# dt*u*B of two or four states a unit made by ScalarE and TensorE, more products with C on GpSimd, and Wout loaded by halves

## The chip, the cores and the metric

The kernel runs on one core of a Trainium2 chip. The metric is the device time of one execution in microseconds. In the text VectorE, ScalarE, GpSimd, TensorE and SyncE are the engines; SyncE only issues the transfers.

## What is computed

For x of 4 batches by 512 positions by 512 features: a layer norm, then `x + mamba(xn) + ffn(xn)`. The part around the change is the state recurrence of mamba, cut here to its core:

```python
dA = exp(A * dt)                  # per channel (1024), position (512) and state n (16)
dBu = (dt * Bm) * hs              # dt*u times B of the state, u = hs
h = dA_t * h + dBu_t              # a scan over the positions
y = sum over n of h * C
y = (y + hs * D) * silu(gate)
out = y @ Wout.T
```

The FFN is a gated one in fp8: `gelu(x@w0) * (x@w1)`, again to fp8, times w_linear.

## The kernel before, in words

There are two stages with a barrier between them. `block_a` makes the layer norm, the projections, the convolution, dt and dt*u, and leaves dt, dt*u and u*D of each unit (128 channels of one batch) in DRAM (`unit_d`), and B and C (`bc_d`). `block_b` runs 32 units, b of 4 by k of 8, in Python loops that are written out in full. A tile is 128 channels by 512 positions. For each of the 16 states n of a unit:

- ScalarE makes exp(A*dt) into one of four PSUM tiles `da[n % 4]` (L887). Before it waits till state n-4 has left that tile: when VectorE has made its product, or, where GpSimd makes it, when the scan is done.
- GpSimd makes dt*u*B into `dbu`, a ring of 8 tiles (L928), up to 8 states ahead of the scans.
- VectorE scans (L985). The result goes in place into `da`, or into `hp` for the states of `POOLED` = 1, 4, 7, 9, 12.
- The product with C is VectorE's (`prod`, L954, made behind the next state's scan) for 11 states, and GpSimd's (`hp` in place, L939, three states behind its dt*u*B) for the 5 of `POOLED`.
- TensorE transposes each product with four 128x128 matmuls and sums them in PSUM (`yT`, L1104), behind a skip term (L1119); GpSimd's products are taken 4 states later (`PE_LAG`).

The rest is placed by hand between the states. ScalarE, at state 6 of the next unit (`SWITCH`), copies yT (L856), makes the Silu of the gate (L877) with a table load on each side; TensorE turns y back (`BACK`, step 4); VectorE multiplies both at state 7 (`GATED`, L960, written y2). TensorE makes the FFN's products (L1062) in steps given by `FFN`, the gate's (L1074), and Wout in two halves of channels: `out_a` (first four units) in units 5 to 7 and `out_b` (last four) in units 0 to 3 of the next batch (L1026). A piece placed at -3 runs ahead of the unit's skip term. TensorE has two banks `mm` for all of them. ScalarE copies the FFN's banks at states 10 to 15 (L895) and makes the Gelu at state 1 of the next unit, between two table loads (L867, L868); VectorE multiplies and clips at state 4 (L1000, L1003), and GpSimd waits for that clip ahead of its product for state 4 (`PORT_GIVEN`), so that it is idle during the two bf16 instructions. VectorE adds out_a and out_b into `acc` (L966, L972) at states given by `OUT_A_ADDED` and `OUT_B_ADDED` (15 in unit 0, 5 in units 1 to 3). Units 1 to 5 have FFN work of that kind on VectorE.

SyncE's queue loads the next unit, the gate's and the FFN's weights while a unit runs, and in unit 7 the B and C tiles of the next batch, each behind a wait for its last reader. Wout is loaded once, 2 MB.

## Time and profile before

| | |
|---|---|
| median of 3 runs | 1150.81 us (1149.45 to 1151.9) |
| the profiled execution | 1151.44 us, its span 1149.7 us |
| VectorE busy | 1041.4 us, 91% |
| GpSimd busy | 926.6 us, 81% |
| TensorE busy (matmuls) | 932.7 us, 81% |
| ScalarE busy | 784.8 us, 68% |
| mean granted TensorE clock | 0.922 |
| first stage, to the barrier | about 240 us |

The page of the profile gives busy time and share for each engine over the span, then groups of instructions with their count, mean duration and the idle time of the engine ahead of them. A busy share is a mean over both stages. A timeline lists the instructions in order of time, several of one kind merged into a row, with the idle time ahead of the row in brackets and what ended it.

### The profile page before, as it was taken

What the parts mean: (1) busy time and instruction counts of PE and PEld (TensorE: products, weight loads), DVE (VectorE), ACT (ScalarE), POOL (GpSimd) and SP (SyncE); (2) the same over time, 40 slices, a digit from 0 to 9 for tenths busy, and PEclk for the clock granted to TensorE, in tenths of its full rate; (3) what the DMA queues carried; (4) which work ended last, traced back from release to release, by engine and by line L of the source; (5) the groups of instructions that cost most, each with busy time, mean ns of one, the idle gap of its engine ahead of it and who ended that gap; (6) DMA issues with size and microseconds to landing.
All of it is one profiled execution on the core that took longest, in us unless ns stands there. A gap on an engine that the chain in (4) does not pass through costs nothing.

```text
span 1149.7 us, 14675 instructions
## 1 busy us (share of the span) xinstructions
PE 932.7 (81%) x4304; PEld 573.4 (50%) x4304; DVE 1041.4 (91%) x1237; ACT 784.8 (68%) x1117; POOL 926.6 (81%) x751
## 2 busy tenths in 40 slices
PE   4979798747777798888887988887988788787988
PEld 3746465424444455555444555554545545454554
DVE  6958778579999999999999999999999999999994
ACT  3878887647777755767785557777846577787551
POOL 5333424389999999989999999999989989999991
PEclk9999999967998899899988998899889899989899
DMA  7566767983111217522212183321213922212100
GB/s 279 204 240 219 266 220 265 341 329 116 51 55 38 83 37 224 206 87 72 80 51 83 43 288 137 116 74 56 83 37 102 326 81 69 74 46 74 37 1 37
DMA packets 53158, 150.24 MB, mean 131 GB/s; under 512 B 5728, under 2 KB 14048, under 8 KB 50016
## 3 DMA queue, kind: packets, MB, share of 16 engines
q1 hardware_dynamic: 53088, 149.41, 37.7%
q8 instruction: 32, 0.52, 0.2%
q14 instruction: 38, 0.31, 0.1%
HBM read 111.37 MB, written 38.01 MB: 130 GB/s over the span
## 4 chain that ended last, share of the span: by engine, by line
POOL 52%; DVE 13%; issue 7%; PE 5%; ACT 0%; DVEq 0%; POOLq 0%
POOL dbu L928 38%; POOL hp L939 14%; DVE da L985 3%; DVE prod L954 3%; DVE hp L985 3%; PE mm L1026 2%; DVE gate_bf L1000 2%; DVE act L1003 2%; PE yT L1104 1%; PE mm L1083 1%; PE da L1026 1%; PE mm L1074 1%; ACT da L887 0%; DVE y L960 0%; ACT gate_bf L895 0%
## 5 line engine op out<-in xcount | busy, mean ns | idle before, releaser
L887 ACT ACTIVATE da<-unit,neg_a 128x512 f32<-128x512 f32 x512 | 340.2, 685 | 263.1 <-DVE prod L954 256.7
L928 POOL TENSOR_TENSOR dbu<-unit,b_head 128x512 f32<-128x512 f32 x384 | 478.0, 1280 | 3.5 <-POOLq L99 3.5
L985 DVE TENSOR_TENSOR_SCAN da<-da,dbu 128x512 f32<-128x512 f32 x352 | 418.3, 1217 | 7.7 <-POOL dbu L928 6.5
L1104 PE MATMUL yT<-ident,prod 128*128 128x128 f32 x1408 | 238.2, 298 | 150.4 <-DVE prod L954 149.8
L1104 PEld LDWEIGHTS yT<-ident,prod 128*128 128x128 f32 x1408 | 174.8, 151 | 282.1 <-DVE prod L954 242.1
L939 POOL TENSOR_TENSOR hp<-hp,c_head 128x512 f32<-128x512 f32 x128 | 163.6, 1278 | 59.0 <-DVE act L1003 45.9
L985 DVE TENSOR_TENSOR_SCAN hp<-da,dbu 128x512 f32<-128x512 f32 x160 | 193.4, 1209 | 7.9 <-ACT da L887 7.9
L954 DVE TENSOR_TENSOR prod<-da,c_head 128x512 f32<-128x512 f32 x256 | 171.3, 669 | 0.0
L928 POOL TENSOR_TENSOR dbu<-unit,b_all 128x512 f32<-128x512 f32 x128 | 160.4, 1280 | 0.0
L1062 PE MATMUL mm<-xn_b,w_sb 128*128 128x512 fp8e4 x512 | 151.6, 432 | 4.4 <-ACT gate_bf L895 3.3
L1074 PE MATMUL mm<-xnT_b,wgate 128*128 128x512 f32 x256 | 127.9, 597 | 1.8 <-ACT gate_bf L895 1.7
L1026 PE MATMUL mm<-y,wout_sb 128*128 128x512 f32 x240 | 111.9, 594 | 0.6 <-ACT gate_bf L895 0.6
L1104 PE MATMUL yT<-ident,hp 128*128 128x128 f32 x640 | 104.5, 290 | 0.0
L286 POOL TENSOR_TENSOR hs_lo<-hs,hs_hi 128x512 fp32r<-128x512 f32 x32 | 43.5, 1363 | 69.5 <-ACT hs_hi L465 69.5
L1062 PEld LDWEIGHTS mm<-xn_b,w_sb 128*128 128x128 fp8e4 x512 | 54.1, 110 | 63.4 <-issue 33.9
L289 POOL TENSOR_TENSOR dt_du<-dt_du,hs 128x512 f32<-128x512 f32 x32 | 41.1, 1284 | 53.8 <-DVE dt_du L405 53.4
L1104 PEld LDWEIGHTS yT<-ident,hp 128*128 128x128 f32 x640 | 82.4, 151 | 0.0
L350 DVE SCALAR_TENSOR_TENSOR conv<-proj,cols_sb,conv 128x511 f32<-128x511 f32 (+2 forms) x96 | 71.5, 747 | 8.8 <-ACT conv L446 6.3
L1083 PE MATMUL mm<-act,w_sb 128*128 128x512 fp8e4 x256 | 71.4, 416 | 0.0
L954 DVE TENSOR_TENSOR prod<-da,c_all 128x512 f32<-128x512 f32 x96 | 64.7, 675 | 0.0
L520 PE MATMUL proj<-xnT_lo,win_hi 128*128 128x512 f32 x128 | 55.8, 436 | 8.2 <-ACT xnT L427 4.3
L1026 PEld LDWEIGHTS mm<-y,wout_sb 128*128 128x128 f32 x240 | 42.9, 190 | 39.1 <-issue 36.7
(107 smaller groups left out, 1248.2 us busy)
## 6 DMA issues: line engine op xcount, KB each, us to landing
unit<-unit_d SPq DMA_DIRECT2D x32, 768.0 KB, 4.3
unit_d<-dt_du SPq DMA_DIRECT2D x32, 512.0 KB, 2.8
wf<-in_wffn SPq DMA_DIRECT2D x12, 1024.0 KB, 5.9
c_head<-bc_d SPq DMA_DIRECT2D x24, 512.0 KB, 5.0
b_head<-bc_d SPq DMA_DIRECT2D x18, 512.0 KB, 5.2
unit_d<-hsd SPq DMA_DIRECT2D x32, 256.0 KB, 3.9
w_sb<-w_d SPq DMA_DIRECT2D x64, 128.0 KB, 3.3
wgate<-in_win_gate SPq DMA_DIRECT2D x32, 256.0 KB, 2.7
```

The costliest lines, as they stand in the source:

```text
L350: ins = nc.vector.scalar_tensor_tensor(out=conv[:, k % 2, back:L], in0=proj[k % 3][:, 0:L - back], scalar=cols_sb[:, k, C_TAP + TAPS - 1 - ...
L520: nc.tensor.matmul(bank, hi, low, start=start, stop=False)
L887: nc.scalar.activation(da[n % SLOTS][:, :], unit[:, k % 2, 0, :], ACT.Exp, scale=neg_a[:, k, n:n + 1]).then_inc(da_ready, 1)
L928: nc.gpsimd.tensor_tensor(dbu[:, n % DBUS, :], unit[:, k % 2, 1, :], b_all[n // NS][:, n % NS, :], ALU.mult).then_inc(dbu_ready, 1)
L939: nc.gpsimd.tensor_tensor(hp[:, i % HPS, :], hp[:, i % HPS, :], c_all[m // NS][:, m % NS, :], ALU.mult).then_inc(hp_ready, 1)
L954: nc.vector.tensor_tensor(prod[:, slot, :], da[n % SLOTS][:, :], c_all[n // NS][:, n % NS, :], ALU.mult).then_inc(prod_ready, 1)
L985: nc.vector.tensor_tensor_scan(state, da[n % SLOTS][:, :], dbu[:, n % DBUS, :], 0.0, ALU.mult, ALU.add).then_inc(scanned, 1)
L1026: return nc.tensor.matmul(bank[:, :], wout_sb[:, c, h * P:(h + 1) * P], y2[:, c, :], start=(c == first), stop=(c == KU // 2 - 1))
L1062: ins = nc.tensor.matmul(bank[:, :], wffn[:, k % 2, j, f, s, :].bitcast(FP8), xn8[:, f, :].bitcast(FP8), start=(f == 0), stop=(f == HT - 1))
L1074: ins = nc.tensor.matmul(bank[:, :], wgate[:, k % 2, c * P:(c + 1) * P], xnT[:, c, :], start=(c == 0), stop=(c == 3))
L1083: ins = nc.tensor.matmul(bank[:, :], wlin[:, i, h * P:(h + 1) * P].bitcast(FP8), act8[:, i, :].bitcast(FP8), start=(i == 0), stop=(i == HI ...
L1104: ins = nc.tensor.matmul(yT[k % 2][:, t * P:(t + 1) * P], product[:, t * P:(t + 1) * P], ident[:, :], start=False, stop=last, is_transpose ...
```

## The change

A class `Ring` counts slots and semaphore values, now that the states of a kind differ from unit to unit. Units 0, 6 and 7 are LIGHT, 1 to 5 HEAVY. In a HEAVY unit GpSimd makes 6 products with C (states 0, 2, 4, 7, 9, 12) and 14 dt*u*B; in a LIGHT one 7 (0, 2, ..., 12) and 12. The dt*u*B of states 8 and 12 (HEAVY) or 4, 7, 10 and 13 (LIGHT) is made another way: TensorE turns dt*u of the next unit (`turn_u`, at its step 11) in the free yT bank, ScalarE copies it to `u_T` behind exp 15, and, one state ahead of each such state, multiplies it with B, which then is a value for each partition, in four 128x128 instructions (`scale_u`); TensorE turns the result into the PSUM tile of the state, four steps ahead (`turn_scaled`). exp(A*dt) of such a state goes to a tile in SBUF (`decay`, two of them) and its scan reads that and the PSUM tile. B turned (`bT_all`) is made at the end of each batch of the first stage. `prod` has 7 tiles for 8, `hp` 6 for 5. Wout has room for one half, and the halves are loaded in turn: the first at unit 4, the second at unit 7 of each batch. The diff, cut:

```diff
@@ -46,15 +46,49 @@
 WINS = 4
 DTS = 4
 SWITCH, GATED, GELU = 6, 7, 1
-DBUS = 8
-POOLED = (1, 4, 7, 9, 12)
-POOL_LAG, PE_LAG = 3, 4
-HPS = 5
-Y, M = len(POOLED), N - len(POOLED)
-OWN = tuple(n for n in range(N) if n not in POOLED)
-PRODS = 8
-ADDED = {n: [m for m in POOLED if min(m + PE_LAG, N - 1) == n] for n in range(N)}
-
+DBUS, PRODS, HPS, DECAYS, SCALED = 8, 7, 6, 2, 1
+POOL_LAG, PE_LAG, Z_AHEAD = 3, 4, 1
+LIGHT, HEAVY = (0, 2, 4, 6, 8, 10, 12), (0, 2, 4, 7, 9, 12)
+POOLED = (LIGHT, HEAVY, HEAVY, HEAVY, HEAVY, HEAVY, LIGHT, LIGHT)
+FEW, MANY = (8, 12), (4, 7, 10, 13)
+BY_SCALE = (MANY, FEW, FEW, FEW, FEW, FEW, MANY, MANY)
+
+
+def others(states):
+    return tuple(tuple(n for n in range(N) if n not in states[k]) for k in range(KU))
+
+
+class Ring:
+
+
+    def __init__(self, states, size):
+        self.states, self.size = states, size
+        self.order = [(k, n) for k in range(KU) for n in states[k]]
+        self.total = len(self.order)
+
+    def slot(self, k, n):
+        return self.order.index((k, n)) % self.size
...
+            return self.order[i - self.size], False
+        return [at for at in self.order if self.slot(*at) == self.slot(k, n)][-1], True
+
+
+OWN, BY_POOL = others(POOLED), others(BY_SCALE)
+PROD, HP, DBU, SCALE = Ring(OWN, PRODS), Ring(POOLED, HPS), Ring(BY_POOL, DBUS), Ring(BY_SCALE, SCALED)
+DECAY = Ring(BY_SCALE, DECAYS)
+ADDED = [{n: [m for m in POOLED[k] if min(m + PE_LAG, N - 1) == n] for n in range(N)} for k in range(KU)]
 
 
...
 FFN, FFN_COPIED = (5, 5, 5, 5, 4), (10, 10, 10, 10, 8)
 OUT_B, OUT_B_ADDED = (11, -3, -3, -3), (15, 5, 5, 5)
 GATE = (12, 11, 11, 11, 12, 12, 12, 10)
+U_T, U_T_COPIED = 11, 15
...
@@ -582,6 +625,14 @@
                     project_dt(k)
                     if k in (2, 5) and not last:
                         project(b + 1, k // 3)
+                if not last:
+                    pe.wait_ge(xnT_ready, b * HT + HT + HT - 1 + 2)
+                else:
+                    pe.wait_ge(bT_copied, B)
+                pe.sem_inc(waited, 1)
+                for t in range(LT):
+                    ins = nc.tensor.transpose(tp[0][:, t * 2 * N:(t + 1) * 2 * N], bc[:, t * P:(t + 1) * P], ident[0:2 * N, 0:2 * N])
+                ins.then_inc(bT_mm, 1)
 
             run_batches(pe, body)
...
@@ -766,6 +833,9 @@
                 sp.dma_start(w8_sb[:, :].rearrange("p (c n) -> p c n", c=HID // P * H // CHUNK),
                              w8_d[HID // P // 2:CHUNKS, :, :].rearrange("c p n -> p c n")).then_inc(wlin_loaded, 16)
 
+            def load_wout(half):
+                sp.dma_start(wout_sb[:, :, :], wout[:, half * KU // 2:(half + 1) * KU // 2, :]).then_inc(wout_loaded, 16)
+
             def load_xnT(b):
                 sp.dma_start(xnT[:, :, :].rearrange("p k l -> p (k l)"), row(xnT_d, b)).then_inc(xnT_loaded, 16)
...
+                if k == HT and not opening and b > 0:
+                    wait(out_b_mm, b * HT + HT)
+                    load_wout(0)
+                if k == KU - 1:
+                    wait(out_a_mm, b * HT + HT)
+                    load_wout(1)
...
         def _(act):
-            def sum_of(u, k):
-
-                act.wait_ge(hp_used, u * Y + Y + HPS)
+            def sum_of(b, k):
+
+                act.wait_ge(hp_used, HP.until(b, k + 1) + HP.total)
                 nc.scalar.activation(y_t[:, :], yT[k % 2][:, :], ACT.Copy).then_inc(y_t_ready, 1)
+
+            def copy_u(u, k):
+
+                act.wait_ge(u_T_mm, u + 1)
+                nc.scalar.activation(u_T[:, :], yT[k % 2][:, :], ACT.Copy).then_inc(u_T_ready, 1)
+
+            def scale_u(b, k, n, opening):
+
+                act.wait_ge(u_T_ready, b * KU + k + 1)
+                act.wait_ge(bT_ready, b + 1)
+                act.wait_ge(*slot_left(SCALE, dbu_mm, b, k, n))
+                for t in range(LT):
+                    ins = nc.scalar.activation(scaled[:, SCALE.slot(k, n), t * P:(t + 1) * P], u_T[:, t * P:(t + 1) * P], ACT.Copy,
+                                               scale=bT[:, t, n:n + 1])
+                ins.then_inc(scaled_ready, 1)
 
             def body(b, k, opening):
                 u = b * KU + k
...
+                    if n == 1 and first:
+                        copy_u(0, 0)
+                    if n == 1 and k == 0:
+                        nc.scalar.activation(bT[:, :, :].rearrange("p (o t) n -> p o t n", o=1),
+                                             bT_all[:, 0:1, :, :] if opening else bT_all[:, bass.ds(b, 1), :, :],
+                                             ACT.Copy).then_inc(bT_ready, 1)
+                    if n + Z_AHEAD in BY_SCALE[k]:
+                        scale_u(b, k, n + Z_AHEAD, opening)
+                    target = da[n % SLOTS][:, :]
+                    if n in BY_SCALE[k]:
+                        target = decay[:, DECAY.slot(k, n), :]
+                        if not (opening and DECAY.before(k, n)[1]):
+                            act.wait_ge(*scanned_before(DECAY, b, k, n))
+                    elif n >= SLOTS:
+                        act.wait_ge(*state_left(b, k, n - SLOTS))
+                    elif k > 0:
+                        act.wait_ge(*state_left(b, k - 1, n - SLOTS + N))
+                    elif not opening:
+                        act.wait_ge(*state_left(b - 1, KU - 1, n - SLOTS + N))
+                    nc.scalar.activation(target, unit[:, k % 2, 0, :], ACT.Exp,
                                          scale=neg_a[:, k, n:n + 1]).then_inc(da_ready, 1)
+                    if n == U_T_COPIED and not (isinstance(b, int) and b == B - 1 and k == KU - 1):
+                        copy_u(u + 1, (k + 1) % KU)
                     if k < FFN_UNITS and 0 <= n - FFN_COPIED[k] < 2 * HIDS[k]:
 
...
-                    nc.gpsimd.tensor_tensor(dbu[:, n % DBUS, :], unit[:, k % 2, 1, :], b_all[n // NS][:, n % NS, :], ALU.mult).then_inc(dbu_ready, 1)
+                    if n in BY_POOL[k]:
+                        if k == 0 and (n % NS == 0 or n - 1 not in BY_POOL[k]):
+
+                            if n >= G_AHEAD * NS:
+                                pool.wait_ge(b_loaded[n // NS], b * 16 + 16)
+                            elif not opening:
+                                pool.wait_ge(b_loaded[n // NS], b * 16)
+                            elif n == 0:
+                                pool.wait_ge(b_head_loaded, 16 * (B - 1))
+                        if not (opening and DBU.before(k, n)[1]):
+                            pool.wait_ge(*scanned_before(DBU, b, k, n))
...
+                        nc.gpsimd.tensor_tensor(dbu[:, DBU.slot(k, n), :], unit[:, k % 2, 1, :], b_all[n // NS][:, n % NS, :],
+                                                ALU.mult).then_inc(dbu_ready, 1)
+                    if 1 <= k <= FFN_UNITS and n == PORT_GIVEN:
+                        pool.wait_ge(act8_ready, b * FFN_UNITS + k)
...
@@ -976,16 +1086,19 @@
                 first = opening and k == 0
                 for n in range(N):
                     dve.wait_ge(da_ready, u * N + n + 1)
-                    dve.wait_ge(dbu_ready, u * N + n + 1)
                     state = da[n % SLOTS][:, :]
-                    if n in POOLED:
-                        i = POOLED.index(n)
-                        dve.wait_ge(hp_used, u * Y + i + 1)
-                        state = hp[:, i % HPS, :]
-                    nc.vector.tensor_tensor_scan(state, da[n % SLOTS][:, :], dbu[:, n % DBUS, :], 0.0,
-                                                 ALU.mult, ALU.add).then_inc(scanned, 1)
-
-                    if n > 0 and n - 1 in OWN:
+                    given = state, dbu[:, DBU.slot(k, n), :] if n in BY_POOL[k] else None
+                    if n in BY_POOL[k]:
+                        dve.wait_ge(dbu_ready, DBU.count(b, k, n))
+                    else:
+                        dve.wait_ge(dbu_mm, SCALE.count(b, k, n) + SCALE.total)
+                        given = decay[:, DECAY.slot(k, n), :], state
+                    if n in POOLED[k]:
...
@@ -1042,6 +1155,22 @@
                     if name != "out_b" and not (opening and wrapped):
                         break
                 return mm[bank]
+
+            def turn_u(b, k):
+
+                pe.wait_ge(unit_loaded[k % 2], unit_loads(b, k))
+                for t in range(LT):
+                    ins = nc.tensor.transpose(yT[k % 2][:, t * P:(t + 1) * P], unit[:, k % 2, 1, t * P:(t + 1) * P], ident[:, :])
+                ins.then_inc(u_T_mm, 1)
+
+            def turn_scaled(b, k, n):
+
+                pe.wait_ge(scaled_ready, SCALE.count(b, k, n))
+                pe.wait_ge(*state_left(b, k, n - SLOTS))
+                for t in range(LT):
+                    ins = nc.tensor.transpose(da[n % SLOTS][:, t * P:(t + 1) * P], scaled[:, SCALE.slot(k, n), t * P:(t + 1) * P],
+                                              ident[:, :])
+                ins.then_inc(dbu_mm, 1)
 
             group_bank = {}
...
+                        pe.wait_ge(prod_ready, PROD.count(b, k, n))
+                        add_state(k, prod[:, PROD.slot(k, n), :], False).then_inc(prod_used, 1)
+                    for m in ADDED[k][n]:
+                        pe.wait_ge(hp_ready, HP.count(b, k, m))
+                        add_state(k, hp[:, HP.slot(k, m), :], m == POOLED[k][-1]).then_inc(hp_used, 1)
+                    if n + SLOTS in BY_SCALE[k]:
+                        turn_scaled(b, k, n + SLOTS)
+                    if n == U_T and not (isinstance(b, int) and b == B - 1 and k == KU - 1):
+                        if not first:
+                            pe.wait_ge(y2_ready, u)
+                        if k < KU - 1:
+                            turn_u(b, k + 1)
+                        else:
+                            turn_u(b + 1, 0)
                     if n == BACK and not first:
                         back(u - 1, (k - 1) % KU)
                     for piece in pieces:
                         beside(b, k, piece, opening)
 
-            pe.sem_inc(prod_used, PRODS)
-            pe.sem_inc(hp_used, HPS)
+            pe.sem_inc(prod_used, PROD.total)
```

The other hunks put the ring's counts where the constant ones were and declare the new tiles and semaphores.

## Rows read from the trace of the kernel before

**Rows 1.** The page, busy time and share of the engines.
```profile
PE 932.7 (81%) x4304; PEld 573.4 (50%) x4304; DVE 1041.4 (91%) x1237; ACT 784.8 (68%) x1117; POOL 926.6 (81%) x751
```
**Rows 2.** The page, groups of instructions: busy us, mean ns | idle before.
```profile
L928 POOL TENSOR_TENSOR dbu<-unit,b_head 128x512 f32<-128x512 f32 x384 | 478.0, 1280 | 3.5 <-POOLq L99 3.5
L985 DVE TENSOR_TENSOR_SCAN da<-da,dbu 128x512 f32<-128x512 f32 x352 | 418.3, 1217 | 7.7 <-POOL dbu L928 6.5
...
L954 DVE TENSOR_TENSOR prod<-da,c_head 128x512 f32<-128x512 f32 x256 | 171.3, 669 | 0.0
```
**Rows 3.** Windows of an FFN unit and of unit 7: engines, clock, DMA.
```profile
core 0: us, PE busy (x) PEld busy (x) DVE busy (x) ACT busy (x) POOL busy (x), PEclk, DMA share, GB/s
...
535.53:563.63 28.10, 22.90 (x114) 14.21 (x112) 27.56 (x33) 21.15 (x29) 25.87 (x22) 0.93 0.23 75
...
672.51:697.78 25.27, 20.58 (x100) 13.11 (x99) 25.15 (x30) 14.75 (x21) 25.27 (x21) 0.84 0.94 336
```
**Rows 4.** Timeline (start, us, engine, ...) of VectorE in an FFN unit.
```profile
530.38 1.22 DVE L985 TENSOR_TENSOR_SCAN da<-da,dbu 128x512 f32<-128x512 f32 x1
...
542.92 0.67 DVE L954 TENSOR_TENSOR prod<-da,c_head 128x512 f32<-128x512 f32 x1
543.50 2.34 DVE L985 TENSOR_TENSOR_SCAN da<-da,dbu 128x512 f32<-128x512 f32 x2
...
550.24 1.23 DVE L985 TENSOR_TENSOR_SCAN hp<-da,dbu 128x512 f32<-128x512 f32 x1 [0.39 <-ACT da L887]
```
**Rows 5.** Timeline of ScalarE in the same unit.
```profile
543.62 0.69 ACT L887 ACTIVATE da<-unit,neg_a 128x512 f32<-128x512 f32 x1 [0.50 <-DVE prod L954]
544.25 0.58 ACT L895 ACTIVATE up_bf<-mm 128x512 bf16<-128x512 f32 x1
...
549.52 1.92 ACT L887 ACTIVATE da<-unit,neg_a 128x512 f32<-128x512 f32 x3
```
**Rows 6.** Timeline of TensorE in the same unit, its step 11.
```profile
544.13 0.60 PE L1104 MATMUL yT<-ident,prod 128*128 128x128 f32 x4
544.57 0.60 PE L1104 MATMUL yT<-ident,hp 128*128 128x128 f32 x4
```
**Rows 7.** Timeline of GpSimd, its wait in the next FFN unit.
```profile
558.74 1.27 POOL L939 TENSOR_TENSOR hp<-hp,c_head 128x512 f32<-128x512 f32 x1 [2.23 <-DVE act L1003]
```
**Rows 8.** Timeline, VectorE's bf16 product beside GpSimd, and without it.
```profile
302.18 3.72 POOL L928 TENSOR_TENSOR dbu<-unit,b_head 128x512 f32<-128x512 f32 x3
...
305.33 1.38 DVE L1000 TENSOR_TENSOR gate_bf<-gate_bf,up_bf 128x1536 bf16<-128x1536 bf16 x1
...
528.41 0.95 DVE L1000 TENSOR_TENSOR gate_bf<-gate_bf,up_bf 128x1536 bf16<-128x1536 bf16 x1
```
**Rows 9.** Timeline of ScalarE and VectorE in unit 0 of a batch.
```profile
686.75 1.21 DVE L985 TENSOR_TENSOR_SCAN hp<-da,dbu 128x512 f32<-128x512 f32 x1
...
689.81 0.58 ACT L856 ACTIVATE y_t<-yT 128x512 f32<-128x512 f32 x1
...
693.00 2.57 DVE L985 TENSOR_TENSOR_SCAN da<-da,dbu 128x512 f32<-128x512 f32 x2
...
693.61 1.91 ACT L887 ACTIVATE da<-unit,neg_a 128x512 f32<-128x512 f32 x3
```
**Rows 10.** Timeline, scan 1 and TensorE's skip term in units 6 and 7.
```profile
635.49 1.21 DVE L985 TENSOR_TENSOR_SCAN hp<-da,dbu 128x512 f32<-128x512 f32 x1
...
641.09 0.60 PE L1119 MATMUL yT<-ident,unit 128*128 128x128 f32 x4
...
661.12 1.21 DVE L985 TENSOR_TENSOR_SCAN hp<-da,dbu 128x512 f32<-128x512 f32 x1
...
665.84 0.60 PE L1119 MATMUL yT<-ident,unit 128*128 128x128 f32 x4
```
**Rows 11.** One tile's instructions: ScalarE's only 128x128 copy.
```profile
L870 ACT ACTIVATE ident_bf<-ident x1: 293/293/293, 246.8 to 246.8; 128x128 bf16<-128x128 f32 x1
```
**Rows 12.** Timeline of VectorE in state 15 of unit 0.
```profile
491.74 0.69 DVE L972 TENSOR_TENSOR acc<-mm,acc 128x512 f32<-128x512 f32 x1 [2.46 <-PE mm L1033]
```

## What I expect, and why

> **What bounds the kernel now.** The table of engines comes first: VectorE is busy for 91% of the span, GpSimd for 81%, TensorE for 81% [rows 1]. Shares over the whole span mix two stages, so the windows by unit come next. A unit of the second stage is 16 states of 128 channels, and I take a unit from one y2 product of VectorE (in state 7) to the next. In a unit with FFN work VectorE is busy 27.56 of 28.10 us, GpSimd 25.87; in the last unit of a batch 25.15 of 25.27 [rows 3]. So a unit takes what VectorE's queue takes, and what the change can give is what it takes off that queue, unless a wait of VectorE grows. The waits are seen in the timeline of one unit. I set T at the start of scan 5, the first instruction behind the FFN's clip: 530.38. The only gap in that unit is 0.39 us ahead of scan 1 of the next one, for an exp of ScalarE [rows 4]. That small row matters most: VectorE and ScalarE are already level there.
>
> Start to start, a product with C costs 0.585 us (542.92 to 543.50; its own record says 0.67 because consecutive ones overlap) and a scan 1.13 (two take 2.34, one 1.21) [rows 2, 4].
>
> **What is taken away.** VectorE makes 11 products a unit before; after it is 10 in five units of a batch and 9 in three. That is 5x1+3x2 = 11 a batch, 44 in all, x0.585 = 25.7 us. GpSimd goes from 21 operations a unit (16+5) to 20 (14+6) or 19 (12+7), at 1.28 us each [rows 2]; it wasn't last, it waits 2.23 us for the clip in every FFN unit [rows 7], so that is worth nothing by itself. With no other change of waits the execution of 1151.44 us would take 1125.7.
>
> **What is added, and on which path.** Each unit gets a turn of dt*u (4 transposes), its copy on ScalarE, and for each scaled state 4 small ScalarE instructions and 4 more transposes. The nearest row for a small ScalarE instruction is one 128x128 copy of 0.29 us [rows 11]; consecutive ones overlap by some 0.07, so four take 0.9 to 1.2 us. I take 1.1. The Trainium skill's page "ScalarE: Activation LUTs", section "Rules for kernel authors", budgets about 0.3 us per ACTIVATE and 0.83 ns for an element. By it a 128-column one is 0.41, four are 1.6 us, and each scaled state that lies on a chain would cost 0.5 us more; the 0.29 us row speaks against that price. Four transposes take TensorE 0.44 us start to start when its clock is full [rows 6].
>
> Four transfers of 512 KB of Wout and more replace one of 2 MB; the first half is asked for a unit ahead of its use, the second at the start of the last unit of a batch, behind out_a, and ahead of the loads of B and C on SyncE's queue. Those loads have a unit to land, so I cost this at 0, up to 1 us a batch if the DMA engines, busy 94% of that unit [rows 3], push a late C tile back.
>
> **Path 1, into units 2 to 5 of a batch (16 times).** ScalarE's exp 15 waits for product 11 of VectorE and starts at 543.62; then copy 5 of the FFN (544.25), exp 0, a table load, the Gelu, a table load, and exp 1 at 549.52, for which scan 1 waits [rows 4, 5]. The change puts the copy of the next unit's dt*u between exp 15 and copy 5. It reads what TensorE turns at its step 11, behind the transposes of product 11. Product 11 ends at 543.59, TensorE takes it up at 544.13 = T+13.75 and a GpSimd product at T+14.19 [rows 6]. The turn of scaled state 12, put into step 8, pushes this by up to 0.44; about 0.35 of it falls into the wait for an FFN bank, so I take 0.09: T+13.84, +0.44, +0.44, and the turn itself 0.60 to its end: T+15.3. The copy then starts at T+15.35 and copy 5 at +0.48, T+15.83, where it was T+13.87. Everything behind it moves by 1.96 us, and scan 1 to T+21.8. VectorE's products between T and scan 1 are as many as before (8), so it has nothing to fill this with. From scan 1 to the clip there are two products instead of three: -0.585. Sum: +1.37 us a unit, 21.9 us in 16. Least possible, with TensorE on time: product 11 at T+13.24, 0.44+0.44+0.60 behind it, minus ScalarE's arrival at T+13.88, plus 0.48, is 1.37, net +0.8. Most: TensorE half a microsecond later, and the collision below: +2.2.
>
> The collision: GpSimd takes products for states 7 and 9 three states behind its dt*u*B, and state 8 is no longer its own. By its operations of 1.23 us from T+0.27 on it is at state 7 at T+4.0 while scan 7 ends at T+4.65, and at state 9 at T+7.2 against T+8.1: 1.8 us of new waits. It then ends its last operation ahead of the FFN wait at about T+27.8, and VectorE's bf16 product starts at T+27.5. In the opening one that overlaps a GpSimd run took 1.38 us; in a later unit, where GpSimd was idle, 0.95 [rows 8]. The page "GPSIMD Engine Reference", section "Specifications", says that the SBUF interfaces are shared and contend with VectorE instructions that have two SBUF inputs, as this one has; rows 8 agree. An overlap of 0.3 is within the error of this walk; it stands in the upper end only.
>
> **Path 2, exp 5 to exp 6.** Between them ScalarE copies y, loads a table, makes a Silu and loads the table back: 689.81 to 693.61, 3.8 us [rows 9]. Before, exp 4 and 5 came at the end of product 0. After, state 0 is GpSimd's and state 1 VectorE's, so exp 5 waits for product 1, behind scan 2. With S the start of scan 1 (686.75 in unit 0): exp 5 at S+2.98, y at 3.6, the tables end at 7.4, the scaling of state 7 takes 1.1, exp 6 0.69: scan 6 at S+9.2. Before it starts at 693.00+2.57-1.21 = S+7.6 [rows 9]. That is +1.6 into unit 0, less one product later on, +1.05, 3 times: 3.2 us. In FFN units the clip lies between and hides this chain (scan 6 there is at S+9.4).
>
> **Path 3, turn of state 4 in units 6 and 7.** Scan 4 now waits for TensorE, which has four out_a pieces and the skip term ahead of step 0. In unit 7 the skip term is at 665.84, with scan 1 at 661.12, S+4.72 [rows 10]; turned at S+5.8, scan 4 starts then, scan 6 at S+9.25 instead of S+8.0: +1.25-0.585 = +0.66, 4 times, 2.6 us. In unit 6 the skip term is at 641.09, S+5.6, [rows 10] because TensorE is behind already; two more turns in unit 5 make it S+6.5, scan 4 S+7.5 instead of S+4.5: +3.0-0.585, and I take +2.2 as some of TensorE's backlog should find a gap: 8.8 us in 4.
>
> **Into unit 1 (3 times).** VectorE waits 2.46 us in state 15 for TensorE's out_b [rows 12]. That covers path 1. TensorE has two to three turns more and one or two products fewer ahead of it, +0.4; one product behind it is gone: -0.2 each, -0.5.
>
> **Start.** Each batch of the first stage gets 4 small transposes and a ScalarE copy (not over the 0.58 us of a 512-column copy [rows 5]), and unit 0 must first turn, copy and scale: +2 together, 0 to 3.
>
> **Sum:** 21.9+3.2+2.6+8.8-0.5+2 = +38 us on 1151.44, that is 1189.4; the median of the three runs shown, 1150.81, lies 0.6 below the profiled one, so 1189. The lower bounds of all terms (16x0.8, 3x0.9, 4x0.5, 4x0.5, 3x-1.1, 0) give +16, 1167; the upper ones (16x2.2, 3x1.5, 4x1.2, 4x3, 3x0.6, 3) +61, 1212.
>
> **Rivals.** (a) *It all hides, and VectorE's queue gets shorter.* For it: the row of 0.39 us is small, and ScalarE is idle 7 us of an FFN unit (21.15 busy of 28.10 [rows 3]). Against it: the idle time lies behind product 11's and earlier waits, not between exp 15 and exp 1. It decides if the copy of dt*u costs path 1 less than 0.585 us net; then 1151-25.7+2 = about 1127. (b) *The floor:* TensorE keeps up and only the inserted work counts, about 1167. (c) *GpSimd and TensorE late:* the bf16 product stands behind GpSimd (0.4 us a time, as in rows 8) and TensorE, given 12 to 20 transposes a unit more, slips in every unit; its clock, 0.93 in the FFN unit and 0.84 in unit 7 [rows 3], would be seen lower. About 1210. (d) *The gains and waits cancel*, or the schedule is as good as unchanged: 1151, within 0.2%.
>
> **Chances.** The forecast, with what lies within 12 us of it, 0.46, (b) 0.20, (c) 0.16, (a) 0.14, (d) 0.04. Slower by over 0.2% (about what can be told from no change here) 0.82, faster 0.14, same 0.04. The range leaves out (a), most of (d) and a tail of (c): 1155 to 1215.
>
> **What would show it.** In the profile after: VectorE's idle time ahead of scan 1 in FFN units near 2.4 us and put down to ScalarE's exp (right: path 1), near 0.4 (wrong, a). ScalarE waiting some 1.4 us for TensorE ahead of the copy of dt*u. Scan 6 of unit 0 waiting 1.7 us for ScalarE; scan 4 of units 6 and 7 waiting 1.5 to 3 for TensorE. VectorE's products 44 fewer. GpSimd's wait for the clip gone in FFN units, waits for scans 7 and 9 new. I am wrong if small ScalarE instructions are far cheaper, or TensorE takes product 11 and the turn up at once and scan 1 hardly moves.

## The result, and the profile after

The changed kernel takes 1205.05 us (median of 4 runs, 1202.71 to 1206.18) against 1151.36 us for the kernel before on the same chip (4 runs, 1149.45 to 1152.67): ratio 1.0465, 95% interval 1.0443 to 1.0487. The profiled execution took 1202.71 us, its span is 1200.9. So the kernel got slower by 53.7 us, and the forecast was +38.

In the fences below "after" is the changed kernel, line numbers are its own. First the page: the table of engines, and of the groups (busy us, mean ns | idle before, releaser) that of the scan with both operands in SBUF and that of the small ScalarE instructions.

```profile
PE 977.2 (81%) x4790; PEld 632.3 (53%) x4800; DVE 1020.4 (85%) x1193; ACT 901.2 (75%) x1509; POOL 879.5 (73%) x707
...
L1099 DVE TENSOR_TENSOR_SCAN da<-da,dbu 128x512 f32<-128x512 f32 x264 | 317.1, 1217 | 42.9 <-ACT da L995 42.9
...
L944 ACT ACTIVATE scaled<-u_T,bT 128x128 f32<-128x128 f32 x352 | 111.4, 388 | 1.9 <-PE da L1171 1.8
```

VectorE has 44 instructions fewer than in rows 1 and is busy 21 us less, GpSimd 47 us less; the span grew all the same, and VectorE's share fell from 91% to 85%. What it gained in work it lost several times over in waits. The view of waits names them (engine, line, releaser: us in all, times, longest):

```profile
POOL hp L1051 <- DVE hp L1099: 112.9, 93, 4.3
ACT u_T L936 <- PE yT L1163: 47.8, 32, 3.5
DVE da L1099 <- ACT da L995: 42.9, 18, 2.7
DVE hp L1099 <- issue: 22.5, 13, 2.7
DVE acc L1082 <- remote: 18.4, 4, 5.5
DVE acc L1076 <- PE mm L1139: 8.7, 4, 2.9
```

VectorE is the engine that sets the time, so it is the DVE lines that count. The first (42.9) is almost all scan 1 of the FFN units (16 waits, 40.4 us). The second ("issue", TensorE's turn in fact) is scan 4 of units 6 and 7 (8 waits, 20.6 us). Of the third, three waits of 4.29 are out_b in unit 0; the fourth, 5.5, stands at the end of the kernel and was the same before. The last is out_a in unit 5. Scan 6 of unit 0, three waits of 2.39, is in none of these lines. GpSimd's 112.9 us are on an engine with time to spare, but they decide when it meets VectorE's bf16 instructions.

**By unit.** A period runs from one y2 product to the next, as in rows 3. From the first y2 product to the last it is 852.45 us before and 906.04 after, +53.6, just what the medians differ by. So the difference lies in the second stage, and it can be added up from the 31 periods:

| period into unit | before | after | forecast, all | measured, all |
|---|---|---|---|---|
| 2 to 4 (12 times) | 27.50 to 28.10 | 29.45 to 30.32 | +16.4 | +23.2 |
| 5 (4) | 29.07 | 30.24 | +5.5 | +4.7 |
| 6 (4) | 26.68 to 28.75 | 29.74 to 30.96 | +8.8 | +9.9 |
| 7 (4) | 25.63 | 26.99 | +2.6 | +5.4 |
| 0 (3, and the end) | 25.27 | 26.32 | +3.2 | +3.4 |
| 1 (3) | 30.77 | 32.89 to 33.48 | -0.5 | +7.0 |
| sum | | | +36.0 | +53.6 |

The last 2 us of the forecast were for the start. The first y2 product starts at 284.36 before and at 282.13 after, but in the kernels below, most with the same first stage, anywhere from 282.5 to 287.5, so one trace can't tell this term.

The windows view of after (stretch, length, busy us of PE, PEld, DVE, ACT and POOL with their instructions, granted clock, DMA share, GB/s): an FFN unit and unit 7, which answer to rows 3, then the periods into units 6 and 1.

```profile
547.94:577.99 30.05, 24.41 (x126) 15.78 (x126) 27.37 (x31) 23.97 (x38) 24.73 (x21) 0.90 0.21 71
695.64:721.96 26.32, 20.05 (x113) 13.93 (x112) 23.93 (x28) 19.47 (x39) 23.84 (x20) 0.88 1.00 393
637.69:668.65 30.96, 28.39 (x135) 18.26 (x136) 25.33 (x29) 20.15 (x39) 23.13 (x20) 0.90 0.11 35
721.96:754.85 32.89, 28.79 (x148) 17.30 (x147) 28.45 (x32) 24.21 (x39) 25.63 (x21) 0.99 0.21 70
```

VectorE, busy 27.56 of 28.10 us before [rows 3], is now busy 27.37 of 30.05: 2.7 us idle in a unit.

**An FFN unit.** The timeline (start, us, engine) of after; scan 5 starts at T = 542.79, and the period is one that answers to rows 4, 5 and 6.

```profile
554.45 1.22 DVE L1099 TENSOR_TENSOR_SCAN hp<-decay,da 128x512 f32<-128x512 f32 x1 [0.17 <-issue]
556.29 0.69 ACT L995 ACTIVATE da<-unit,neg_a 128x512 f32<-128x512 f32 x1 [0.77 <-DVE prod L1063]
557.74 0.60 PE L1163 MATMUL yT<-ident,unit 128*128 128x128 f32 x4
558.38 0.60 ACT L936 ACTIVATE u_T<-yT 128x512 f32<-128x512 f32 x1 [1.40 <-PE yT L1163]
558.87 0.59 ACT L1005 ACTIVATE up_bf<-mm 128x512 bf16<-128x512 f32 x1
564.87 1.23 DVE L1099 TENSOR_TENSOR_SCAN da<-da,dbu 128x512 f32<-128x512 f32 x1 [2.36 <-ACT da L995]
570.54 1.28 DVE L1113 TENSOR_TENSOR gate_bf<-gate_bf,up_bf 128x1536 bf16<-128x1536 bf16 x1
```

Exp 15 ends, ScalarE then waits 1.40 us for TensorE's turn of dt*u, copies it, and only then makes FFN copy 5: at T+16.08 where it was at T+13.87 [rows 5]. Scan 1 waits 2.36 us where it waited 0.39 [rows 4]. The bf16 product takes 1.28 us, near the 1.38 beside GpSimd in rows 8, and not 0.95. One sign that the prediction named did not come: GpSimd still waits for the clip in the FFN units, 2.10 us in this one, since the late scan 1 makes the clip late too.

**Unit 7 and unit 0.** Scan 1 of unit 7, TensorE's out_a, skip term and turn of scaled state 4 in unit 7, and the scan that waits for it; then scan 6 of unit 0, and further on in unit 0 FFN copy 5, the gate product that waits for it, and VectorE at out_b; last GpSimd and VectorE's clip in unit 1 (rows 9, 10 and 12 are those of before).

```profile
682.86 1.22 DVE L1099 TENSOR_TENSOR_SCAN da<-da,dbu 128x512 f32<-128x512 f32 x1
...
684.81 3.60 PE L1139 MATMUL mm<-y,wout_sb 128*128 128x512 f32 x8
...
688.24 0.60 PE L1248 MATMUL yT<-ident,unit 128*128 128x128 f32 x4
688.68 0.60 PE L1171 MATMUL da<-ident,scaled 128*128 128x128 f32 x4
689.37 1.22 DVE L1099 TENSOR_TENSOR_SCAN hp<-decay,da 128x512 f32<-128x512 f32 x1 [2.46 <-issue]
...
719.11 1.22 DVE L1099 TENSOR_TENSOR_SCAN hp<-da,dbu 128x512 f32<-128x512 f32 x1 [2.39 <-ACT da L995]
...
732.95 0.60 ACT L936 ACTIVATE u_T<-yT 128x512 f32<-128x512 f32 x1 [2.23 <-PE yT L1163]
733.44 0.59 ACT L1005 ACTIVATE up_bf<-mm 128x512 bf16<-128x512 f32 x1
734.09 1.13 PE L1203 MATMUL mm<-xnT_b,wgate 128*128 128x512 f32 x2 [0.31 <-ACT up_bf L1005]
...
738.92 0.69 DVE L1082 TENSOR_TENSOR acc<-mm,acc 128x512 f32<-128x512 f32 x1 [4.29 <-remote]
...
745.74 3.23 POOL L1039 TENSOR_TENSOR dbu<-unit,b_head 128x512 f32<-128x512 f32 x2
...
747.99 1.79 DVE L1116 TENSOR_SCALAR act<-gate_bf 128x1536 fp8e4<-128x1536 bf16 x1
```

The wait at out_b, 2.46 us in rows 12, is 4.29. The word "remote" only says that no releaser was found; out_b's last product ends at 738.66, 0.26 ahead of the sum.

The sum of out_b splits the period into unit 1 in two. It stands 16.96 us behind y2 (17.54 in one batch) where it stood 15.06. From there to the next y2 it takes 15.93 us for 15.70, although a product with C is gone: the clip takes 1.79 us for the 0.96 of before, because GpSimd is still at work. GpSimd goes on only behind the first scan after out_b, and has six operations from there to its own wait for the clip, where it had four.

### The profile page after: what moved, and what is told of

Same layout as the page of the kernel before. It is cut to its first block, busy times and chain, and to the rows that moved or that the text cites. A ratio compares the mean times of both kernels' runs of the same rounds, so it can differ in the third digit from the quotient of the medians.

```text
span 1200.9 us, 16165 instructions
## 1 busy us (share of the span) xinstructions
PE 977.2 (81%) x4790; PEld 632.3 (53%) x4800; DVE 1020.4 (85%) x1193; ACT 901.2 (75%) x1509; POOL 879.5 (73%) x707
## 4 chain that ended last, share of the span: by engine, by line
PE 27%; DVE 18%; ACT 14%; issue 13%; POOL 7%; another core or an unknown queue 1%; DVEq 1%; ACTq 0%; POOLq 0%
PE yT L1234 9%; DVE da L1099 6%; PE mm L1191 6%; DVE prod L1063 5%; DVE hp L1099 4%; POOL dbu L1039 4%; PE mm L1203 3%; PE mm L1212 3%; POOL hp L1051 3%; ACT da L995 2%; ACT gate_bf L957 2%; PE da L1171 2%; PE mm L1139 2%; ACT L958 2%; ACT L957 2%
## 5 line engine op out<-in xcount | busy, mean ns | idle before, releaser
L1039 POOL TENSOR_TENSOR dbu<-unit,b_head 128x512 f32<-128x512 f32 x328 | 412.0, 1278 | 6.9 <-POOLq L135 3.5
L995 ACT ACTIVATE da<-unit,neg_a 128x512 f32<-128x512 f32 x424 | 285.5, 684 | 161.2 <-DVE prod L1063 154.1
L1099 DVE TENSOR_TENSOR_SCAN da<-da,dbu 128x512 f32<-128x512 f32 x264 | 317.1, 1217 | 42.9 <-ACT da L995 42.9
L1051 POOL TENSOR_TENSOR hp<-hp,c_head 128x512 f32<-128x512 f32 x172 | 218.7, 1271 | 154.7 <-DVE hp L1099 112.9
L1063 DVE TENSOR_TENSOR prod<-da,c_head 128x512 f32<-128x512 f32 x212 | 141.3, 666 | 0.0
L1039 POOL TENSOR_TENSOR dbu<-unit,b_all 128x512 f32<-128x512 f32 x96 | 119.8, 1271 | 0.0
L944 ACT ACTIVATE scaled<-u_T,bT 128x128 f32<-128x128 f32 x352 | 111.4, 388 | 1.9 <-PE da L1171 1.8
L1171 PE MATMUL da<-ident,scaled 128*128 128x128 f32 x352 | 63.4, 310 | 41.2 <-ACT scaled L944 41.1
L1099 DVE TENSOR_TENSOR_SCAN hp<-decay,da 128x512 f32<-128x512 f32 x44 | 53.1, 1207 | 22.6 <-issue 22.5
L1171 PEld LDWEIGHTS da<-ident,scaled 128*128 128x128 f32 x352 | 46.3, 158 | 48.5 <-ACT scaled L944 48.5
```

Source lines behind the costliest of these rows:

```text
L944: ins = nc.scalar.activation(scaled[:, SCALE.slot(k, n), t * P:(t + 1) * P], u_T[:, t * P:(t + 1) * P], ACT.Copy, scale=bT[:, t, n:n + 1])
L995: nc.scalar.activation(target, unit[:, k % 2, 0, :], ACT.Exp, scale=neg_a[:, k, n:n + 1]).then_inc(da_ready, 1)
L1039: nc.gpsimd.tensor_tensor(dbu[:, DBU.slot(k, n), :], unit[:, k % 2, 1, :], b_all[n // NS][:, n % NS, :], ALU.mult).then_inc(dbu_ready, 1)
L1051: nc.gpsimd.tensor_tensor(tile, tile, c_all[m // NS][:, m % NS, :], ALU.mult).then_inc(hp_ready, 1)
L1063: nc.vector.tensor_tensor(prod[:, PROD.slot(k, n), :], da[n % SLOTS][:, :], c_all[n // NS][:, n % NS, :], ALU.mult).then_inc(prod_ready, 1)
L1099: nc.vector.tensor_tensor_scan(state, given[0], given[1], 0.0, ALU.mult, ALU.add).then_inc(scanned, 1)
```

## Experiments

The theory after the result: most of the loss is the place of the copy of dt*u (behind exp 15, ahead of FFN copy 5). Rivals: the small instructions themselves, GpSimd's and TensorE's new order, the halves of Wout. Diffs are against the changed kernel.

**1. The copy of dt*u earlier.** dt*u is turned at TensorE's step 8 and copied in state 14; a wait keeps the copy behind the last use of the old one.

```diff
-U_T, U_T_COPIED = 11, 15
+U_T, U_T_COPIED = 8, 14
...
```

> The changed kernel, with the turn of the next unit's dt*u at TensorE's step 8 (was 11) and its copy behind exp 14 (was 15), where ScalarE has room; a wait for ScalarE's own last scaling goes with it. Theory (path 1, the copy stands in the chain product 11, exp 15, copy, Gelu, exp 1): scan 1's wait of 2.36 us in FFN units falls to 0.4 to 0.6, and units into 2 to 5 from 30.05 to about 28.2; with some of the same in the others some 30 us less, 1175. Rival (GpSimd is next): with scan 1 on time VectorE's bf16 product comes 1.8 us earlier and meets GpSimd, takes 2 us for 0.95, units stay at 29.0 or more, 1188. Rival (ScalarE simply has too much work): no change, 1205.

1172.81 us, ratio 1.0188 (1.0152 to 1.0223): 32 us of the 54 are gone. Into units 2 and 3 it mostly takes 28.48 us for 30.05, into unit 4 27.87 for 29.46, into unit 1 31.88 for 32.89. The timeline of an FFN unit:

```profile
548.13 0.58 ACT L936 ACTIVATE u_T<-yT 128x512 f32<-128x512 f32 x1
556.09 1.23 DVE L1101 TENSOR_TENSOR_SCAN da<-da,dbu 128x512 f32<-128x512 f32 x1 [0.40 <-ACT da L995]
560.11 2.50 POOL L1041 TENSOR_TENSOR dbu<-unit,b_head 128x512 f32<-128x512 f32 x2
561.75 1.67 DVE L1115 TENSOR_TENSOR gate_bf<-gate_bf,up_bf 128x1536 bf16<-128x1536 bf16 x1
```

The copy waits for nothing, and scan 1 is back at 0.40. But VectorE now reaches the bf16 product while GpSimd is at work until 562.61, and the product takes 1.67 us. In most FFN units it is even 1.93 to 1.97 (1.78 in the mean of all of this size), so 0.7 to 1.0 us over 0.95 [rows 8] go there, more than the product with C that was saved (0.585). That half of the rival written down for this run came true.

**2. and 3. Turn and copy alone, late and early.** The products with C, GpSimd's share and all dt*u*B are as in the kernel before; only the turn of dt*u and its copy (whose result nobody uses) and the halves of Wout stay, once at the places of the change, once at those of experiment 1.

```diff
-LIGHT, HEAVY = (0, 2, 4, 6, 8, 10, 12), (0, 2, 4, 7, 9, 12)
-FEW, MANY = (8, 12), (4, 7, 10, 13)
+LIGHT, HEAVY = (1, 4, 7, 9, 12), (1, 4, 7, 9, 12)
+FEW, MANY = (), ()
...
```

> The changed kernel with no scaled states and the old split of products (GpSimd: states 1, 4, 7, 9, 12; 16 dt*u*B), so the kernel before plus the turn and copy of dt*u (which nothing reads), B turned, and Wout by halves. Theory: path 1 alone, +1.96 us in each of 16 FFN units, +31 and a few us in other units, about 1186. Rival (the cost comes with the small ScalarE instructions and the turned products): under +10, below 1161.

> The run with turn and copy alone, these at step 8 and behind exp 14. Theory (only their place costs): FFN units back to 28.1, the 37 us to under 5, about 1153. Rival (TensorE's or ScalarE's added work itself): above 1165.

Late: 1187.95 us, ratio 1.0315 (1.0278 to 1.0352). Early: 1152.27 us, 1.0021 (1.0009 to 1.0032). The late one's timeline:

```profile
558.72 0.60 ACT L936 ACTIVATE u_T<-yT 128x512 f32<-128x512 f32 x1 [1.33 <-PE yT L1163]
565.21 1.22 DVE L1099 TENSOR_TENSOR_SCAN hp<-da,dbu 128x512 f32<-128x512 f32 x1 [2.29 <-ACT da L995]
571.48 0.94 DVE L1113 TENSOR_TENSOR gate_bf<-gate_bf,up_bf 128x1536 bf16<-128x1536 bf16 x1
```

With experiment 1 this makes a square: the late place costs 36 us (1187.95 less 1152.27) without the rest of the change, 32 us with it. A turn and a copy, 0.44 us of TensorE and 0.5 of ScalarE, cost 1.9 us in each FFN unit where they are waited for (29.99 for 28.10 us) and nothing where they are not (28.10). The late run shows path 1 alone, without the collision: here the bf16 product takes 0.94. Turn and copy were moved together. In the rows shown the late place is a wait of 1.3 to 1.4 us for the turn plus 0.5 us of copy; an early turn with the copy left behind exp 15 was not run.

**4. The halves of Wout alone.** Turn and copy are gone too.

> As the run with turn and copy alone, but without the turn and copy too: the kernel before with Wout by halves and B turned in the first stage. Theory: nothing of it is on the path, within 2 us of before (1151). Rival: the 1 MB transfer in unit 7 pushes the loads of B and C back, up to 1 us a batch and a wait of VectorE or GpSimd for a DMA in unit 0.

1151.42 us, 1.0017 (0.9998 to 1.0035), periods as before to 0.03 us, but for one into unit 6. Costing it at 0 was right.

**5. State 7's scaling moved to state 8** in units 0, 6 and 7, so that ScalarE makes exp 6 ahead of it.

```diff
-FEW, MANY = (8, 12), (4, 7, 10, 13)
+FEW, MANY = (8, 12), (4, 8, 11, 14)
```

> The changed kernel with scaled states 4, 8, 11, 14 instead of 4, 7, 10, 13 in units 0, 6 and 7, so no scaling stands between ScalarE's exp 5 and exp 6. Theory (path 2): the wait of scan 6 in unit 0, 2.39 us, falls by the 1.17 us of the scaling, into unit 0 26.32 to about 25.15; units 6 and 7 hardly gain, as scan 4 waits there for TensorE. Some 4 us less, 1201. Rival (the wait is for product 1, wherever the scaling stands): into unit 0 stays 26.3.

1207.08 us, 1.0481 (1.044 to 1.0521): no gain. Scan 6 of unit 0 waits 1.22 us for 2.39, 1.17 less, which is what four small instructions hold ScalarE up, and the period into unit 0 is 25.52 for 26.32. But into unit 1 it takes 33.1 to 34.5 us for 32.9, and into unit 7 27.20 for 26.99. Path 2 is confirmed, and what it gives back is lost ahead of out_b, which TensorE ends. There the turn of state 14 stands right ahead of out_b's first product, which in the shortest of the three periods starts 9.23 us behind y2 for 9.05; what makes the other two over 1 us longer still was not separated.

**6. Fewer scaled states in units 0 and 5.**

```diff
-BY_SCALE = (MANY, FEW, FEW, FEW, FEW, FEW, MANY, MANY)
+BY_SCALE = ((4, 10, 13), FEW, FEW, FEW, FEW, (9, 12), MANY, MANY)
```

> The changed kernel with unit 0's scaled states 4, 10, 13 (7 left out) and unit 5's 9, 12 (8 moved), so TensorE doesn't wait at step 3 or 4 of these units for a scaling that stands behind ScalarE's Silu switch. Theory (what I missed: that wait holds the FFN pieces, and with them out_b in unit 0 and out_a in unit 5): unit 0's first FFN piece starts 2.9 us ahead of y2 again (0.8 in the changed kernel), into unit 1 32.9 to about 31.0, into unit 0 26.3 to 25.2, into unit 6 30.1 to about 28.5; some 17 us less, 1188. Rival (out_b is late because of the turns' own time on TensorE): into unit 1 stays above 32, 1198 or more.

1201.38 us, 1.0445 (1.0419 to 1.047). Into unit 0 it is 25.16, as said. My theory for units 1 and 6 fell: TensorE starts the first FFN piece earlier, and the period into unit 1 stays 32.90, that into unit 6 29.7 to 30.1 where I expected 28.5. The timeline shows why (FFN pieces, then the gate product, out_b's sum):

```profile
725.49 1.02 PE L1191 MATMUL mm<-xn_b,w_sb 128*128 128x512 fp8e4 x4 [0.68 <-ACT up_bf L1005]
...
727.75 1.02 PE L1191 MATMUL mm<-xn_b,w_sb 128*128 128x512 fp8e4 x4 [0.80 <-ACT gate_bf L1005]
...
733.86 1.12 PE L1203 MATMUL mm<-xnT_b,wgate 128*128 128x512 f32 x2 [0.32 <-ACT up_bf L1005]
...
738.69 0.69 DVE L1082 TENSOR_TENSOR acc<-mm,acc 128x512 f32<-128x512 f32 x1 [4.29 <-remote]
```

TensorE waits for banks that ScalarE copies out, and the last of these copies stands behind the copy of dt*u. So into unit 1 it is the same late copy again, and experiments 1, 2 and 3 size it: late alone 31.77 against 30.77 (+1.0), early alone 31.25 (+0.5), all of the change 32.89 (+2.1), all with the copy early 31.88 (+1.1). Of 2.1 us the place is 1.0 (0.5 where the rest of the change is absent), turn and copy at an early place 0.5. The other 0.6 comes with the rest of the change, in two parts: 0.4 ahead of out_b's sum, and 0.2 behind it, where the clip beside GpSimd costs 0.83 and the product saved gives back 0.585. In experiments 2 and 3 the clip takes 0.96.

**7. No scaled state 4 in units 6 and 7.**

```diff
+BY_SCALE = (MANY, FEW, FEW, FEW, FEW, FEW, (7, 10, 13), (7, 10, 13))
```

> The changed kernel with units 6 and 7's scaled states 7, 10, 13 (4 left out). Theory (two chains end at the same time there, TensorE's turn of state 4 and ScalarE's exp 6): in unit 6 the wait of scan 4, 2.69 us, goes, but scan 6 then waits for exp 6, so into 6 gains about 1.3 us; in unit 7 the gain is under 0.3 us. 5 us less, 1200. Rival (the turn of state 4 alone is the limit): both gain in full, into 7 from 26.99 to 25.8, 10 to 15 us less.

1200.93 us, 1.0442 (1.0419 to 1.0465). Into unit 7 it is 26.32 for 26.99, more than I expected, and still 0.7 over before. Into unit 6 it is 0.75 us less in the mean of the four, where I expected 1.3. The row says what came in its place, scan 6 in unit 7:

```profile
690.06 1.22 DVE L1099 TENSOR_TENSOR_SCAN hp<-da,dbu 128x512 f32<-128x512 f32 x1 [1.78 <-ACT da L995]
```

That is path 2, which I had counted in unit 0 only: units 6 and 7 have it as well, under the wait for state 4.

**8. Early copy, two scaled states and six GpSimd products in every unit.**

```diff
-LIGHT, HEAVY = (0, 2, 4, 6, 8, 10, 12), (0, 2, 4, 7, 9, 12)
-FEW, MANY = (8, 12), (4, 7, 10, 13)
+LIGHT, HEAVY = (0, 2, 4, 7, 9, 12), (0, 2, 4, 7, 9, 12)
+FEW, MANY = (8, 12), (8, 12)
...
```

> The run with the early copy, with units 0, 6 and 7 made like the others: states 8 and 12 scaled, GpSimd's products 0, 2, 4, 7, 9, 12. So state 4 is not turned and nothing is scaled between exp 5 and exp 6. Theory (paths 2 and 3 and the extra turns in units 0 and 6 make what is left of the loss): into 6 29.3 to about 27, into 7 26.76 to 25.3, into 0 26.31 to 25.3, into 1 31.88 to 31.2, the FFN units stay at 28.5; 18 us less, about 1155. Rival (exp 5's wait for product 1 is what counts in units 6 to 0): into 7 and into 0 stay above 26, 1165.

1170.78 us, 1.0179 (1.0162 to 1.0196), a miss. Units 7 and 0 are near before (25.82), but scan 6 of unit 0 still waits 1.22 us, since exp 5 stays behind product 1, and the bf16 product still takes 1.80 in the mean. Into unit 1 it got worse, 32.7 to 33.6. That can't be read from out_b's wait, which is 3.31 us here and 3.28 in experiment 1: its sum stands 16.8 to 17.6 us behind y2 for 15.94, since TensorE is later, and VectorE is held up ahead of it as well (scan 12 waits 0.78 us for a turn in the shortest one).

**9. GpSimd's products one state later.** Experiment 8, and GpSimd takes a product 4 states behind its dt*u*B, TensorE 5; two of the six are of other states.

```diff
-POOL_LAG, PE_LAG, Z_AHEAD = 3, 4, 1
+POOL_LAG, PE_LAG, Z_AHEAD = 4, 5, 1
+LIGHT, HEAVY = (0, 2, 4, 6, 9, 11), (0, 2, 4, 6, 9, 11)
...
```

> The run before this one, with GpSimd's products one state later (lag 4, taken by TensorE 5 states later) and of states 0, 2, 4, 6, 9, 11. Theory (in FFN units GpSimd loses time in waits for scans 7 and 9 and so meets VectorE's bf16 product): the waits go, that product falls from 1.78 to about 0.95, units into 2 and 3 from 28.48 to 27.9, 10 us less, about 1145 and faster than the kernel before. Rival (the bf16 product is slow for another cause): it stays at 1.8 and the units at 28.5.

1165.79 us, 1.0144 (1.0124 to 1.0164), 5 us less than experiment 8 and far from the 1145 expected. Here an FFN unit, its bf16 product and GpSimd's wait for the clip:

```profile
557.48 0.95 DVE L1115 TENSOR_TENSOR gate_bf<-gate_bf,up_bf 128x1536 bf16<-128x1536 bf16 x1
...
559.71 1.27 POOL L1053 TENSOR_TENSOR hp<-hp,c_head 128x512 f32<-128x512 f32 x1 [2.43 <-DVE act L1118]
...
564.01:591.58 27.57, 21.97 (x120) 14.81 (x119) 26.94 (x32) 23.97 (x39) 24.66 (x21) 0.87 0.25 86
```

The collision is gone, GpSimd waits 2.43 us for the clip as in rows 7, and the unit takes 27.57 us, 0.53 less than before: the product with C that the change takes away is, at last, a gain, all but 0.05 us of it. The periods into units 5, 6, 7 and 0 lost some 8 us together against experiment 8.

**10. All of it together.** GpSimd's products in the light units begin with state 1, the scaled states are 9 and 12.

```diff
+LIGHT, HEAVY = (1, 3, 5, 7, 9, 11), (0, 2, 4, 6, 9, 11)
+FEW, MANY = (9, 12), (9, 12)
...
```

> The run with early copy and GpSimd lag, with states 9 and 12 scaled in all units and, in units 0, 6 and 7, GpSimd's products 1, 3, 5, 7, 9, 11, so exp 5 again follows product 0. Theory: FFN units stay at 27.6, into 1 falls from 32.0 to 31, into 6 from 29.5 to 27.5, into 7 and 0 from 26.1 to 25.1; 1143 to 1148, faster than before. Rival (TensorE's added turns alone keep out_a and out_b late): into 1 and 6 stay, 1158.

1150.8 us against 1150.75, ratio 0.9998 (0.9984 to 1.0013, 12 runs): no difference that can be measured, where 1143 to 1148 was expected. Into units 2 and 3 it is mostly 27.58, into 7 25.04, into 0 24.66, all 0.5 to 0.6 below before; into 1 30.9 to 31.7 and into 6 27.8 to 30.4 take it back.

**11. States 9 and 13 in place of 9 and 12** in experiment 10.

> The same with states 9 and 13 scaled. The turn of state 13 is at step 9 instead of 8, between the last two FFN pieces. Theory: within 2 us of the run with 9 and 12; if TensorE's queue in steps 8 to 11 decides, up to 3 us apart.

1161.4 us, 1.0087 (1.0065 to 1.0108), 10.6 us more for one state moved by one, where at most 3 was expected. Its timeline:

```profile
548.07 0.60 PE L1173 MATMUL da<-ident,scaled 128*128 128x128 f32 x4
...
548.78 1.23 DVE L1101 TENSOR_TENSOR_SCAN da<-decay,da 128x512 f32<-128x512 f32 x1 [1.62 <-PE da L1173]
```

The view of waits has 17.7 us in 18 such waits: the turn of state 13 stands in TensorE's step 9. The scaling was done at 544.44, so it isn't what the turn waited for. Ahead of it TensorE had here, without a pause, the turn of dt*u (546.34), an FFN piece (546.77) and a product of GpSimd (547.64). With state 12 the turn is in step 8 and ahead of the first two.

**12. One scaled state fewer in units 0 and 5** of experiment 10.

```diff
+BY_SCALE = ((12,), FEW, FEW, FEW, FEW, (12,), FEW, FEW)
...
```

> The version with everything put together, but in units 0 and 5 of a batch only state 12 is scaled and turned; GpSimd makes dt*u*B of state 9 there. Theory (TensorE's turns are what makes these two units long, since out_b and out_a wait behind them): scan 9's wait of 0.8 to 1.0 us for the turn in unit 0 is gone, the periods into unit 1 (30.9 to 31.7) and into unit 6 (27.8 to 30.4) are 0.5 to 1 us shorter each, nothing else moves: 3x0.6+4x0.7 = 4.6 us, 1146 us, ratio 0.996. Rival (the products of out_a and out_b wait for banks that ScalarE copies, and a turn only fills a gap): the wait for the turn becomes a longer one at out_b, periods as in the version put together, 1151 us, ratio 1.000. A second rival: one dt*u*B more for GpSimd in these units puts it behind the bf16 product again, slower, 1153.

1151.77 us, 1.0016 (1.0002 to 1.003): the 1146 was a miss, the rival's 1151 came. The scan that waited for a turn is that of state 12, not 9 as I wrote: ahead of it come y2, scans 8 to 11 and two products (0.6+4x1.13+2x0.585 = 6.3 us behind the start of y2, as the timeline of experiment 10 has it). In unit 0 the wait is gone and into unit 1 it takes 0.1 to 0.7 us less (30.74, 31.22, 30.76). Into unit 6 nothing is won, it takes 30.0 to 30.4 us in all four batches. The windows view of these periods: two of the kernel before, two of experiment 10, one of this one, and below them three single microseconds of this one.

```profile
397.19:425.77 28.58, 26.96 (x121) 16.09 (x120) 26.32 (x31) 14.75 (x21) 26.11 (x23) 0.87 0.10 38
620.20:646.88 26.68, 25.06 (x121) 15.01 (x120) 26.32 (x31) 14.75 (x21) 26.10 (x23) 0.95 0.12 40
```
```profile
614.74:645.11 30.37, 28.50 (x136) 18.79 (x135) 26.51 (x31) 16.76 (x29) 24.88 (x21) 0.87 0.11 35
1060.41:1088.21 27.80, 25.93 (x136) 16.80 (x135) 26.42 (x32) 16.86 (x29) 24.91 (x21) 0.96 0.13 39
```
```profile
617.41:647.77 30.36, 27.64 (x132) 17.90 (x131) 26.51 (x31) 17.08 (x30) 26.04 (x22) 0.87 0.12 35
...
612.00:613.00 1.00, 0.00 (x0) 0.00 (x0) 1.00 (x2) 0.99 (x3) 0.00 (x0) 1.00 0.00 0
...
618.00:619.00 1.00, 0.39 (x2) 0.00 (x0) 1.00 (x2) 0.90 (x4) 1.00 (x2) 0.50 0.00 0
...
626.00:627.00 1.00, 1.00 (x8) 0.72 (x7) 1.00 (x2) 0.91 (x2) 1.00 (x2) 1.00 0.00 0
```

The same work takes 26.7 or 28.6 to 28.8 us in the kernel before, 27.8 or 29.6 to 30.4 in experiment 10, and each time the longer one has the lower granted clock. In unit 5 TensorE waits 4.84 us for VectorE's product (4.88 in the kernel before); within that wait the clock goes to 0.50 (1.2 GHz) and stays there for 6.8 or for 10.2 us in these periods (10.2 in all four of this experiment), then it is back at 1.00 (2.4 GHz). The timeline of the last one, before and behind that change:

```profile
616.42 1.12 PE L1236 MATMUL yT<-ident,prod 128*128 128x128 f32 x4 [4.84 <-DVE prod L1065]
...
626.39 0.60 PE L1236 MATMUL yT<-ident,hp 128*128 128x128 f32 x4
```

Four transposes take 1.1 us for 0.60 while it is low. Then come FFN products and out_a, back to back to the end of the unit, and out_a is what VectorE waits for. So in this unit 3.4 us more at the low clock are worth 1.8 to 2.6 us, and which it will be isn't in the kernel's order alone: one execution has both. This is where experiment 10's last microseconds hang; no run here steers it.

## Why the prediction was right, and where it was off

The direction, the engine that bounds and the two main paths came out; the sum was 16 us short. 1205 is inside the range, but outside the 12 us around the forecast that had a chance of 0.46, and nearer to rival (c), 1210. By the periods 17.6 us are missing; 6.8 of them are path 1's into units 2 to 4 and 7.5 the periods into unit 1.

**Path 1** was right as a mechanism: waits, releaser and order are as told, and experiments 1 to 3 show that the place of the copy alone makes it. Its size was low, +1.95 us and not +1.37 into units 2 to 4. The two halves of the step tell where. To scan 1: T+22.08 for the T+21.8 of the forecast, because TensorE takes product 11 up at T+14.08. I had put it at T+13.84: the turn of state 12 was to move it by 0.09 only, and it moved by 0.33. The FFN piece behind that turn starts 0.96 us later than before (T+11.05 for T+10.09), and the wait for a bank takes up only part of it. The wait of 0.17 us of scan 12 in the fence above, which makes product 11 0.26 us late, isn't the cause: the period before has no such wait, and its turn, copy and scan 1 stand as far behind y2, to 0.02 us. Behind scan 1: -0.27 for -0.585, because the bf16 product took 1.28 us for 0.95. I had seen that collision, found an overlap of 0.3 us "within the error of this walk", and put it into the upper end; it happened in all 16 periods into units 2 to 5. Into unit 5 it was +1.17, a little less than said. **The rivals** (a) and (b) fell: ScalarE's idle time is not where the copy stands, and TensorE does not keep up. (c) named the right additions, at about the right total (1210), but over the span the clock hardly moved, 0.917 for 0.922; it is seen to matter into unit 6 only.

**Path 2** was exact, +1.05 us into unit 0, with a wait of 2.39 us for 1.7. The failed step is its count: I costed it 3 times, for unit 0. Units 6 and 7 have the same table loads between exp 5 and 6, and there it stands under the wait for state 4 (experiment 7: without that wait still +0.69).

**Path 3**: scan 4 waits for TensorE as told (2.46 and 2.69 us, forecast 1.5 to 3), but costs 1.36 us into unit 7 and not 0.66. With S the start of scan 1 (682.86), I put the skip term at S+4.72, where it was, and scan 4 at S+5.8; TensorE gets to out_a at S+1.95, where it was at S+1.28, has the skip term at S+5.38, and scan 4 starts at S+6.51. These 0.7 us are the difference. Into unit 6 the sum, +9.9 for +8.8, is in part right for a wrong reason: 1.15 us a batch, 4.6 in all, remain where both kernels have the same 10.2 us at the low clock (29.75 against 28.6 us). Most of the rest is that two periods of before had 6.8 us of it and one of after 13.7; whether the change makes that likelier is open.

**Into unit 1** is the step that failed: forecast -0.2, measured +2.1 to +2.7. The prediction said that the wait at out_b "covers path 1". It does cover VectorE's side, but the end of that wait is TensorE's, and TensorE's products wait for banks which ScalarE copies behind the copy of dt*u (experiment 6). A wait covers only what isn't upstream of its own releaser. I counted TensorE's added turns there (+0.4) and not its waits: the sum of out_b came 1.9 us later behind y2, 2.5 in one batch. Behind it I took off a product (-0.585) and measured +0.2, since the clip beside GpSimd takes 0.83 us more; the prediction had no collision for the clip.

**Small instructions.** I took 0.29 us from a copy of the same shape [rows 11] and 1.1 us for four. They take 388 ns each and 1.26 to 1.28 us for four, start of the first to end of the last. The Trainium skill's page "ScalarE: Activation LUTs", section "Rules for kernel authors", budgets about 0.3 us and 0.83 ns an element, an estimate of 0.41 for one; this case's rows are within 6% of it, though four of them, which overlap, come to 1.27 and not 1.6. The copy, to bf16 and without a scale from memory, was the wrong neighbour, but the sum hardly felt it: 0.1 to 0.2 us on each chain.

**Wout's halves** at 0 and 44 products fewer were right; the start can't be told.

## What to carry to other kernels

When an instruction is put into the queue of an engine that is level with the bound one, its price is the time until its input is ready plus what stands behind it, not its own length: the same turn and copy cost 37 us at one place and some 2 us where the turn stood three steps and the copy one state earlier (experiments 2 and 3, each against the kernel before). A wait that seems to cover a delay covers it only if its releaser doesn't depend on the delayed instruction, so follow the releaser one engine further before writing a zero. And freeing the bound engine moves the others against each other: the product saved was worth 0.53 of its 0.585 us only after the copy had moved and GpSimd's products had been moved too.

## What the runs showed of the hardware

VectorE's bf16 product of 128x1536 takes 0.95 us alone. Where it begins with more than 0.1 us of a GpSimd f32 operation still to run, it ends 0.81 or 0.82 us after that operation's end, whenever it began: at 306.71 for 305.90 in rows 8, 571.82 for 571.00 in the changed kernel, 563.42 for 562.61 in experiment 1. So it took 1.28 to 1.97 us in the periods of the second stage that met it, and more at that stage's start (4.15 in experiment 10), where GpSimd's operations follow each other. The clip did the same: 749.78 for 748.97, 1.79 us for 0.96. The other way round, a GpSimd operation that began inside the product was held, so that two of dt*u*B took 3.23 us for 2.50. VectorE's f32 products and scans, with one operand in PSUM, took their 0.67 and 1.2 us beside GpSimd too.

And the stretch at TensorE's low clock behind the same idle time isn't the same each time: in a unit that TensorE bounds at its end, periods with the same instructions differ by 1.8 to 2.6 us within one execution, 6.8 against 10.2 us at 1.2 GHz.
